# Ternary weights of the last stage made in pieces beside the first attention, kept as bf16 and loaded transposed during the second attention

## The reference, cut to what matters

```
def _ternary_quant(w):                       # w1, w2: (2048, 512)   w3: (512, 2048)
    s = mean(abs(w))                         # one number for the whole matrix
    wq = round(tanh(w / (s + 1e-8))) * arctanh(s)
def _linear_bit(x, w, g):
    xq = _act_quant(_rmsnorm(x, g))          # g multiplies the normed row
    return einsum('bsd,od->bso', xq, _ternary_quant(w))
y = linear_bit(silu(linear_bit(x, w1, g1)) * linear_bit(x, w2, g2), w3, g3)
```

## Time and profile before

| stage | from, us | length, us | TensorE busy, us | granted clock |
|---|---|---|---|---|
| attention0_stage | 45.3 | 1116.5 | 1066.2 | 0.99 |
| ffn0_front_stage | 1161.8 | 276.8 | 257.0 | 0.90 |
| experts_stage | 1438.6 | 232.0 | 219.5 | 0.98 |
| attention1_setup_stage | 1670.6 | 46.5 | 30.2 | 0.76 |
| attention1_stage | 1717.1 | 174.4 | 130.0 | 0.90 |
| ffn1_setup_stage | 1891.5 | 65.0 | 21.9 | 0.55 |
| ffn1_stage | 1956.5 | 242.9 | 200.8 | 0.93 |

### The profile page before, as it was taken

The page is one execution under the profiler, slowest core; times in us unless marked ns, Lnnn a source line. Parts: engine busy times, 40 slices in busy tenths (PEclk is TensorE's granted clock), DMA queues, the critical chain, the costliest instruction groups (busy, mean ns, idle before and its releaser), DMA issues. The chain is left out here.

```text
span 2199.4 us, 29096 instructions
## 1 busy us (share of the span) xinstructions
PE 1941.4 (88%) x9804; PEld 1390.7 (63%) x9842; DVE 1074.6 (49%) x2218; ACT 1069.8 (49%) x2269; POOL 963.6 (44%) x904
## 2 busy tenths in 40 slices
PE   3899999999999999999997999999995688338998
PEld 2576666667666676676656777689994466224443
DVE  4344443444334443344435476234433687557886
ACT  2445454444545444444543211156661576647775
POOL 1644454434544355444421000078882355116774
PEclk9999999999999999999997999999997799659999
DMA  4100000000000000000004100358877400100000
GB/s 124 45 20 1 11 29 21 1 1 10 29 21 1 1 10 30 1 1 1 1 1 152 48 20 15 122 169 231 231 186 205 153 1 1 77 30 15 20 20 25
DMA packets 71224, 114.40 MB, mean 52 GB/s; under 512 B 7825, under 2 KB 35345, under 8 KB 70369
## 3 DMA queue, kind: packets, MB, share of 16 engines
q1 hardware_dynamic: 63904, 95.68, 13.0%
q0 software_dynamic: 7168, 16.78, 3.7%
HBM read 91.48 MB, written 22.02 MB: 52 GB/s over the span
## 5 line engine op out<-in xcount | busy, mean ns | idle before, releaser
L585 POOL TENSOR_TENSOR a_xcl<-xT,a_xch 128x512 fp32r<-128x512 f32 x64 | 82.4, 1288 | 475.9 <-ACT a_xch L454 475.9
L524 DVE TENSOR_REDUCE a_nmax<-a_S 128x1 f32<-128x192 f32 (+3 forms) x256 | 139.3, 555 | 253.6 <-PE a_S L660 251.4
L716 PE MATMUL a_A<-a_pT,a_vf 128*128 128x512 f32 (+1 forms) x448 | 234.9, 606 | 1.4 <-ACT a_pT L467 1.2
L659 PE MATMUL a_S<-a_kT,a_qT 128*128 128x288 f32 (+3 forms) x640 | 212.9, 431 | 3.0 <-ACT a_pr_even L457 1.8
L457 ACT ACTIVATE a_pr_odd<-a_S,a_nmax 128x320 f32<-128x320 f32 (+1 forms) x128 | 81.0, 634 | 178.3 <-DVE a_nmax L524 176.6
L467 ACT ACTIVATE a_pT<-a_TR 128x512 f32<-128x512 f32 (+1 forms) x224 | 133.1, 595 | 62.1 <-PE a_TR L706 62.1
L117 PE MATMUL a_A<-a_wlo,a_xch 128*128 128x512 f32 x256 | 152.0, 594 | 10.5 <-DVE a_qb L547 9.4
L659 PEld LDWEIGHTS a_S<-a_kT,a_qT 128*128 128x128 f32 x640 | 120.5, 191 | 54.7 <-issue 27.1
L457 ACT ACTIVATE a_pr_even<-a_S,a_nmax 128x192 f32<-128x192 f32 (+1 forms) x128 | 67.0, 526 | 152.8 <-DVE a_nmax L524 152.7
L678 PE MATMUL a_A<-a_wkv,xT 128*128 128x256 f32 x512 | 136.6, 391 | 0.6 <-DMA a_wkv<-in_L_xattn_wv_dram 0.6
L1315 POOL TENSOR_TENSOR e_wlo<-expert_raw,e_whi 128x1408 fp32r<-128x1408 f32 x32 | 103.5, 3252 | 68.4 <-ACT e_whi L1388 68.4
(11 more groups left out here) (379 smaller groups left out, 5073.5 us busy)
## 6 DMA issues: line engine op xcount, KB each, us to landing
expert_raw<-in_L_ffn_w_gate_dram SPq DMA_DIRECT2D x16, 704.0 KB
expert_raw<-in_L_ffn_w_up_dram SPq DMA_DIRECT2D x16, 704.0 KB
expert_raw<-in_L_ffn_w_down_dram SPq DMA_DIRECT2D x16, 512.0 KB
ffn_raw<-in_L_ffn_w_dram SPq DMA_DIRECT2D x4, 2048.0 KB
x_res<-in_x_dram SPq DMA_DIRECT2D x4, 1024.0 KB
a_raw<-in_L_xattn_wq_dram SPq DMA_DIRECT2D x4, 1024.0 KB
a_raw<-in_L_xattn_wo_dram SPq DMA_DIRECT2D x4, 1024.0 KB
xn_rows<-xg SPq DMA_DIRECT2D x16, 256.0 KB, 2.0
```

What stands on the lines that cost most here:

```text
L524: ve.tensor_reduce(nmax[:, s % 2, i:i + 1], pair(s, i), AX.X, ALU.max, negate=True).then_inc(s_max, 1)
L585: pool.tensor_tensor(xcl[:, t % 2], xT[:, :, tok(t)], xch[:, t % 2].bitcast(F32), ALU.subtract).then_inc(xlo_ready, 1)
L659: pe.matmul(bank[:, lo:hi], qT[:, t % 2, hq], kT[:, par(t), lo:hi], start=True, stop=hi < nk)
L716: last = pe.matmul(A[:, A_USE["V", t, 0][0]], vf[r, par(t), i], pT[r, i % 2], start=i == 0, stop=i == nkt - 1)
```

## The change

1. `ffn1_setup_stage` and `ffn_load` are gone.
2. In `attention0_stage` the loop is gone: all slots from -4 to 65 are written out, and every wait compares with a constant.
3. ScalarE gets three pieces of absolute sums in each of 16 slots (2 to 11 and 16 to 21), 48 pieces of 128 x 512, placed behind e0, behind g0, and ahead of e3. VectorE gets the totals in slots 22 and 23 and, in 24 slots (24 to 27, 32 to 43, 48 to 55), two ternary pieces of 128 x 512 each, behind D and ahead of M3. Totals over partitions are made by a store to DRAM and a load that broadcasts them. SyncE's program is written out by slots: it loads each piece (two buffers, each piece twice: once for the sum, once for the comparison), stores each ternary piece as bf16 to DRAM, and in between loads the group weights as before.
4. `attention1_setup_stage` now holds the chain that makes `at` (eight small VectorE operations and one logarithm on ScalarE, at the end of both queues), and rounds in place instead of into `wi`.
5. In `attention1_stage` SyncE brings the three bf16 matrices from DRAM with `dma_start_transpose` (2 MB each) and the three g by broadcast, and waits for all.
6. In `ffn1_stage` the scaling of g is done by ScalarE at the head of its queue, ahead of its wait for `const_ready`.

```diff
-    ACT_ORDER = ("w x e0 e1 g0 e2 v g1 n g2 e3 g3 k t g4 o f",
+    ACT_ORDER = ("w x e0 j0 e1 g0 j1 e2 v g1 n g2 j2 e3 g3 k t g4 o f",
...
-    DVE_ORDER = ("M0 M1 N0 D M2 N1 v N2 M3 N3 B E",
+    DVE_ORDER = ("M0 M1 N0 D j0 M2 N1 v N2 j1 M3 N3 B E",
...
     def walk(eng, order, do):
-        for s in range(BEGIN, LOOP):
+        for s in range(BEGIN, END):
             for name, i in steps(order, s):
                 do(name, i, s, None)
-        with eng.Fori(0, KVH - 1) as m:
-            for s in range(LOOP, LOOP + PERIOD):
...
+    SUM_SLOTS = [*range(2, 12), *range(16, 22)]
+    TOTAL_SLOT = 22
+    TERN_SLOTS = [*range(24, 28), *range(32, 44), *range(48, 56)]
...
+                def load_piece(k):
+                    j, o = k % PIECES // FFN_PIECES, k % FFN_PIECES
+                    if k < 2 * PIECES:
+                        sp.dma_start(pw[:, k % 2], piece(j, o)).then_inc(piece_loaded[k % 2], 16)
+                def store_tern(n):
+                    sp.dma_start(tern_piece(n // FFN_PIECES, n % FFN_PIECES), tern[:, n % 2]).then_inc(tern_stored[n % 2], 16)
...
+                        if (s, i) in SUMS:
+                            n = SUMS[s, i]
+                            sp.wait_ge(piece_used, n + 1)
+                            if n + 2 < PIECES:
+                                load_piece(n + 2)
...
+                    if name == "j" and (s, i) in SUMS:
+                        k = SUMS[s, i]
+                        act.wait_ge(piece_loaded[k % 2], 16 * (k // 2 + 1))
+                        act.activation(tern[:, k % 2], pw[:, k % 2], ACT.Abs, accum_out=sabs[:, k:k + 1]).then_inc(piece_used, 1)
...
+                        ve.wait_ge(piece_loaded[u], 16 * (k // 2 + 1))
+                        ve.tensor_scalar(below[:], pw[:, u], nthr[:, j:j + 1], None, ALU.is_lt).then_inc(below_ready, 1)
+                        ve.wait_ge(below_ready, n + 1)
+                        if n > 1:
+                            ve.wait_ge(tern_stored[u], 16 * (n // 2))
+                        ve.scalar_tensor_tensor(tern[:, u], pw[:, u], thr[:, j:j + 1], below[:], ALU.is_gt, ALU.subtract).then_inc(piece_used, 1)
...
+                act.wait_ge(u_ready, 1)
+                act.activation(lnu[:], u[:], ACT.Ln).then_inc(ln_ready, 1)
...
+            def turn_weights(sp, turned):
+                for w, d in zip((*w12T, w3T), tern_dram):
+                    sp.dma_start_transpose(w[:], d).then_inc(turned, 16)
+                sp.dma_start(g12[:, 0], a["L1_ffn_g1"].partition_broadcast(P)).then_inc(turned, 16)
+                sp.dma_start(g12[:, 1], a["L1_ffn_g2"].partition_broadcast(P)).then_inc(turned, 16)
+                sp.dma_start(g3[:], a["L1_ffn_g3"].partition_broadcast(P)).then_inc(turned, 16)
+                sp.wait_ge(turned, 96)
...
+                act.activation(g12[:], g12[:], ACT.Copy, scale=-127.0).then_inc(const_ready, 1)
+                act.activation(g3[:], g3[:], ACT.Copy, scale=127.0).then_inc(const_ready, 1)
```

More of the change, by code:

```diff
@@ L58 @@
 F1 = 2048
+FFN_N = float(F1 * D)
+ROUND_UP = 0.5493061443340549
+FFN_PIECES = F1 * D // (P * 512)
 BIG = 1536.0
@@ L277, in walk, with piece, tern_piece @@
     def walk(eng, order, do):
-        for s in range(BEGIN, LOOP):
+        for s in range(BEGIN, END):
             for name, i in steps(order, s):
                 do(name, i, s, None)
-        with eng.Fori(0, KVH - 1) as m:
-            for s in range(LOOP, LOOP + PERIOD):
[L283 to L287, removed]
+    PIECES = 3 * FFN_PIECES
+    SUM_SLOTS = [*range(2, 12), *range(16, 22)]
+    TOTAL_SLOT = 22
+    TERN_SLOTS = [*range(24, 28), *range(32, 44), *range(48, 56)]
+    SUMS = {(s, i): 3 * n + i for n, s in enumerate(SUM_SLOTS) for i in range(3)}
+    TERNS = {(s, i): 2 * n + i for n, s in enumerate(TERN_SLOTS) for i in range(2)}
+    def piece(j, o):
+        w = ffn_in[j]
+        return w[o * P:(o + 1) * P, :] if j < 2 else w[o // 4 * P:(o // 4 + 1) * P, o % 4 * 512:(o % 4 + 1) * 512]
+    def tern_piece(j, o):
+        w = tern_dram[j]
+        return w[o * P:(o + 1) * P, :] if j < 2 else w[o // 4 * P:(o // 4 + 1) * P, o % 4 * 512:(o % 4 + 1) * 512]
     def tile(t):
@@ L376, in attention0_stage @@
         c_ms, c_rs, c_ready = s_.sem("c_ms"), s_.sem("c_rs"), s_.sem("c_ready")
+        piece_loaded = [s_.sem(f"piece_loaded{u}") for u in range(2)]
+        tern_stored = [s_.sem(f"tern_stored{u}") for u in range(2)]
+        piece_used, below_ready, total_ready, total_stored, total_loaded, mean_ready = (s_.sem(n) for n in (
+            "piece_used", "below_ready", "total_ready", "total_stored", "total_loaded", "mean_ready"))
         SPLIT = KEYS // 2
@@ L420, in _ @@
                 load_pair(0, wkv, wk_in, wv_in, wkv_loaded)
[L421 to L431, removed]
+                load_piece(0)
@@ L433, in _ @@
+                for u in range(2):
+                    sp.wait_ge(tern_stored[u], 16 * (PIECES // 2))
             @block.scalar
@@ L2062, in ffn1_stage @@
-def ffn1_stage(nc, x, ident, gates, g1_in, g2_in, g3_in, w12T, w3T, at, out):
+def ffn1_stage(nc, x, ident, gates, g12, g3, w12T, w3T, at, out):
     PE_ORDER = "P0 P1 U0 P2 U1 P3 T0 Y0"
@@ L2379, in build @@
         gates = sb(ctx, "gates", [P, 4])
+        mean, at = sb(ctx, "mean", [P, 3]), sb(ctx, "at", [P, 3])
+        tern_dram = [nc.dram_tensor(f"tern{j}", shape, BF16).ap() for j, shape in enumerate(((F1, D), (F1, D), (D, F1)))]
+        total_dram = nc.dram_tensor("totals", (P, 3), F32).ap()
         constants_stage(nc, ident, causal, tri, gates, consts, a["g_xattn"], a["g_ffn"])
@@ L2406, in build @@
             experts_stage(nc, ident, xn_dram, y_dram, *weights, raw, loaded, ids, slot_weight, xg, gathered, eo, added)
-        with ExitStack() as weights, ExitStack() as layer:
+        with ExitStack() as weights:
+            w12T = [weights.enter_context(nc.sbuf_tensor(f"w12T{j}", [P, KD, F1], BF16, side="right")) for j in range(2)]
+            w3T = weights.enter_context(nc.sbuf_tensor("w3T", [P, F1 // P, D], BF16, side="right"))
+            g12 = weights.enter_context(nc.sbuf_tensor("g12", [P, 2, D], F32, side="right"))
+            g3 = weights.enter_context(nc.sbuf_tensor("g3", [P, F1], F32, side="right"))
+            def turn_weights(sp, turned):
[5 more added lines that the diff above has]
+                sp.wait_ge(turned, 96)
             with ExitStack() as att:
@@ L2416, in build @@
                                        a["L1_xattn_wv"], a["L1_xattn_bv"], a["L1_xattn_wo"], a["L1_xattn_bq"], a["L1_xattn_bo"],
-                                       a["mask_BxSxS2_ff0"], wT, sq, bq, gsw, gbo, mask, kbd, vbd, x, y_dram, added)
-                bridge.close()
-                raw = layer.enter_context(nc.sbuf_tensor("ffn_raw", [P, 2, F1 * KD], F32, side="right"))
-                loaded = [layer.enter_context(nc.semaphore(f"ffn_loaded{j}")) for j in range(3)]
-                attention1_stage(nc, x, ident, wT, sq, bq, gsw, gbo, mask, kbd, vbd,
-                                 lambda sp: ffn_load(sp, raw, loaded, a["L1_ffn_w1"], a["L1_ffn_w2"]))
-            w12T = [sb(weights, f"w12T{j}", [P, KD, F1], BF16) for j in range(2)]
-            w3T = sb(weights, "w3T", [P, F1 // P, D], BF16)
-            at = sb(weights, "at", [P, 3])
-            ffn1_setup_stage(nc, ident, raw, loaded, a["L1_ffn_w3"], w12T, w3T, at)
-            layer.close()
-            ffn1_stage(nc, x, ident, gates, a["L1_ffn_g1"], a["L1_ffn_g2"], a["L1_ffn_g3"], w12T, w3T, at, out)
+                                       a["mask_BxSxS2_ff0"], wT, sq, bq, gsw, gbo, mask, kbd, vbd, x, y_dram, added, mean, at)
+                attention1_stage(nc, x, ident, wT, sq, bq, gsw, gbo, mask, kbd, vbd, turn_weights)
+            ffn1_stage(nc, x, ident, gates, g12, g3, w12T, w3T, at, out)
 def host_constants():
```

209 lines of the change are left out of this document (73 added, 136 removed), and 12 rows, old and new, of tables (ACT_ORDER, DVE_ORDER).

## The result

The changed kernel takes 2140.93 us (median of 4 runs, 2139.91 to 2143.95), the kernel before in the same session 2201.06 (2200.6 to 2202.58). The ratio is 0.9728 with a 95% interval from 0.9711 to 0.9745. It is faster by 60.1 us. It lies 15.6 us above the forecast of 2125.3, at the slow edge of the range (2115 to 2142) and outside the forecast case (2118 to 2131).

What follows compares the result with a forecast made beforehand. The prediction took TensorE to bound the first attention and the weight stage to be an uncovered serial stretch. Its terms, -65.0 - 6.4 + 1.8 - 8.4 + 2.0 = -76.0, took 2201.3 us to 2125.3, range 2115 to 2142.

Steps and rivals of the forecast that it cites:

- forecast case: Whole kernel: a time of 2118 to 2131 us, given 66%.
- signs of being wrong: Listed waits of TensorE or ScalarE, a longer second attention, more table loads; above all a stretch growing over 15 us.
- Point 1: Weight stage: it goes with its barrier, its work moved or replaced; -65.0 us.
- Point 2: Start of the last stage: first row statistics at about +3.0 us instead of +9.4; -6.4 us.
- Point 3: End of the second attention's setup: table load, logarithm and one product for `at` follow the last copy; +1.8 us.
- Point 4: First attention: written out, two loop-start intervals should take 18.25 us each; -8.4 us.
- Point 5: Pieces beside the first attention: all fit gaps, overruns vanish within slack; +2.0 us, bounds 0 and +92.
- Point 6: Transposing loads during the second attention: hidden, cost 0; estimated 24 us by the skill's 261 GB/s.
- first rival: Transposes outlast the second attention and the last stage waits; 2266 us at 20 GB/s; chance 7%.
- third rival: First attention: written-out stalls cancel the loop's 8.4 us, late loads or delayed maxima cost 2 to 10; 2134 to 2142; chance 20%.

Runs made afterwards that it cites:

- e6: e1 with the chain for `at` and its logarithm moved from the end to the head of the second attention's setup stage: 2117.10 us.
- e4: The kernel before with three engines' walk over the first attention's slots written out, SyncE's loop kept: 2192.03 us against 2200.27.
- e1: The changed kernel with ternary pieces in slot kinds 0, 2 and 3 moved ahead of M3 and of B, where GpSimd is idle: 2120.68 us.
- e5: The changed kernel with both ternary passes replaced at the same places by a tensor_reduce (maximum over 512 columns): 2118.54 us.
- e12: The kernel before with two unused tensors of 12 bytes a partition at the place of mean and at: 2196.95 us against 2200.87.

## Why the prediction was right, and where it was off

The direction and the large term were right, and the time fell inside the range. That it did is partly luck. The forecast case missed, and two of the prediction's own signs of being wrong came: TensorE waits for the rotated keys in slots 24 to 55, and the first attention grew by more than 15 us.

Measured in the profiles of both kernels, spans 2199.4 and 2141.8:

**Point 1** (-65.0): -65.0. Right.

**Point 2** (-6.4): -6.4, the stage going from 243.3 to 236.9 us. The first statistics run 3.4 us behind the start of that stretch, against 9.8 (1965.92 - 1956.1), and from them to the end both kernels take 233.5 us. Right: ScalarE's two scalings took 1.06 and 1.89 us, where I had 2.9 together, and VectorE waits for them (2.36).

**Point 3** (+1.8): +1.1 between the two profiles. The table load (1.28 us) did come behind the last copy, and the chain costs 2.0 us there: 2.9 us from the last copy's end to the next stage after, 0.9 before and in e6. The profiles show less since the last copy itself came 0.9 us earlier, which the chain does not explain.

**Point 4** (-8.4): -5.7 by e4. The mechanism was right, the reading too narrow. I compared one interval from D to D with its counterpart in the written-out tail, 18.25 us, and that one held no fall of the clock. From slot 14 to 18 the kernel before takes 383.01 - 308.08 = 74.93 us, from 30 to 34 76.02, and from 46 to 50, in the tail, 925.69 - 853.73 = 71.96. In the changed kernel the first is 380.29 - 308.49 = 71.80, and the last interval in it 19.62 and not 18.25. Each of these four-slot stretches has TensorE at the lower clock somewhere. In the tail it is 3.4 us (at 860.0, behind a wait of 1.85 us for the keys), three slots ahead of the 18.25. In the changed kernel it is 3.4 us at 375.5, inside the 19.62. At the loop's start it is 6.8 us, behind the wait of 4.32:

```profile
375.40:382.00 6.60, 5.63 (x12) 3.71 (x13) 0.95 (x3) 2.67 (x7) 6.52 (x7) 0.50 0.09 12
```

The loop's start so costs the longer wait and a longer spell at 1.2 GHz, 7.0 us for the two boundaries together. And written out, two of the four kinds of interval take 0.05 to 0.09 us longer (17.05 for 16.99, 16.15 for 16.08; 17.22 and 15.50 stay), some 20 times, which gives 1.3 back; these rows I had before me in the tail. The three rows of before that were missing:

```profile
308.08 0.75 DVE L536 SCALAR_TENSOR_TENSOR x_res<-a_A,gates,x_res 128x512 f32<-128x512 f32 x1 [0.37 <-PE a_A L119]
580.41 0.75 DVE L536 SCALAR_TENSOR_TENSOR x_res<-a_A,gates,x_res 128x512 f32<-128x512 f32 x1 [0.37 <-PE a_A L119]
853.73 0.75 DVE L536 SCALAR_TENSOR_TENSOR x_res<-a_A,gates,x_res 128x512 f32<-128x512 f32 x1 [0.37 <-PE a_A L119]
```

**Point 5** (+2.0) is the term that was mis-sized: +23.0, the first attention's 1133.8 us (from its first instruction) against the 1110.8 of e4. TensorE's wait for the rotated keys, which the point had vanish in 0.4 us of slack, is 19.6 us of it; two more spells of 3.4 us at the lower clock than e4 has from 300 us on come to about as much as the rest. Its sentence "together 1.3 us a piece" took both durations from rows in which GpSimd read nothing that collided, and so did "a gap of 0.93 us for a piece of 1.3. M2 [...] some 0.35 us late". The passes that stand behind D take 1.4 + 1.6 us in half of the slots and 0.55 + 1.6 in most of the others. The rest of point 5 held: each piece of 1.2 to 1.4 us that isn't caught does vanish in the gaps (e1, e5), ScalarE's sums took 0.62 us, and the loads, landing after a median of 2.8 us, were never waited for. The bounds, 0 to +92, held it.

The Trainium skill has the rule, and I did not weigh it: "SBUF — State Buffer", "Who interferes with whom", says that a VectorE instruction with two SBUF inputs, or a tensor_scalar in one of its two-port modes, contends with GpSimd for a port pair that is locked for a whole instruction, and that whoever starts first holds it. These runs agree: slowed are L607 (a tensor_scalar) and L611 (pw and below both in SBUF), to 1.38 and 1.63 us; not slowed are D, whose second tensor is in PSUM, the reduces of e5 (0.68), and GpSimd's product over 128 x 640, which had started first. Its product over 128 x 192, which started second, took 0.95 us. That the port is the cause is the page's account; the runs show who waits for whom, and for how long.

**Point 6** (0): hidden. The three transposes were issued from 1731.16 to 1755.82, and the second attention took 174.2 us. The estimate of 24 us by the skill's figure in "DMA: Bandwidth & Descriptors" was near: all had landed 27 us after the first was issued, 235 GB/s for 6.3 MB. The first rival, with its one descriptor for each element, is out: 24,720 packets of under 512 bytes were moved there, where the values are 3.1 million.

What no point had: ffn0_front, -4.2 us, from where the new tensors push the others (e12, -3.9). With it the terms add up: -65.0 - 6.4 + 1.1 - 5.7 + 23.0 - 4.2 = -57.2, and the spans say -57.6. The time is that of the third rival ("loop and pieces give less", 2134 to 2142), but not by its terms: the loop gave 5.7 us and not nothing, and the pieces cost 23 and not 2 to 10, by a collision that it did not name. Without the 4.2 us of ffn0_front, which were chance, the time would have been about 2145, outside the range.

## What to carry to other kernels

A gap on VectorE isn't free for every instruction: before work is put into it, look at what GpSimd does in the same microseconds, and at whether both read SBUF. The order in the queue decided 20 us here, at no change in work.
When one interval is compared with another, sum over the whole period around it and look at the granted clock in both: here the short interval was one that a spell at 1.2 GHz had missed, and that spell lay three slots earlier.
When a stage that a diff doesn't touch changes by a per cent, look at the spacing of its matmuls, at their clock and at where the tensors lie before giving the credit to the change.

## What the runs showed of the hardware

- VectorE's passes over 128 x 512 values took 0.47 and 0.75 us alone and 1.4 and 1.6 us beside a GpSimd tensor_tensor of 128 x 640; with half the columns 1.25 and 1.43. GpSimd, which had started first, kept its 1.55 us; its 128 x 192 product, started inside VectorE's pass, took 0.95 us in place of 0.505.
- TensorE's matmuls of 512 columns into two of ffn0_front's three tiles came every 0.227 us with the tensors of the changed kernel, every 0.233 with everything 64 bytes nearer or 32 nearer or 32 further: 2.5%, and 3 us in a stage of 263. Which operand decides, the runs don't tell.
- Behind a wait of TensorE of 4.3 us the granted clock was 0.50 for 6.8 us, and for 3.4 us behind some waits of 1.5 to 1.9 us, but not behind all of them.
- A transposing load of 2.1 MB held SyncE's queue for 7.9 to 8.6 us. Nothing stood behind it here but the g.
- Code written out made two of the four kinds of slot 0.05 to 0.09 us longer than in a loop, but saved 3 to 4 us at each of the loop's two boundaries.
